# An inverse transform along W cut into four 64x64 products, with its sums and differences formed one stage earlier and its row sums on GpSimd

## The reference

```python
# x: (4, 128, 128, 768) f32; 8 channel blocks of 96; w1, w2: (2, 8, 96, 96); b1, b2: (2, 8, 96)
xf = jnp.fft.rfft2(x, axes=(1, 2), norm='ortho')            # 128 x 65 modes
o1r = relu(xr @ w1[0] - xi @ w1[1] + b1[0])                 # per mode and block
o1i = relu(xi @ w1[0] + xr @ w1[1] + b1[1])
o2r = softshrink(o1r @ w2[0] - o1i @ w2[1] + b2[0], 0.01)
o2i = softshrink(o1i @ w2[0] + o1r @ w2[1] + b2[1], 0.01)
out = jnp.fft.irfft2(o2r + 1j * o2i, s=(128, 128), axes=(1, 2), norm='ortho') + x
```

## Time and profile before

| | |
|---|---|
| runs of the kernel | 5120.54, 5124.18, 5125.72 us, median 5124.18 |
| profiled execution | span 5120.9 us (the profile gives no other time for it) |
| TensorE, its weight loads | busy 5023.2 us (98%), 4143.8 us (81%) |
| VectorE | 3992.9 us (78%) |
| ScalarE | 2512.6 us (49%) |
| GpSimd | 626.9 us (12%) |
| DMA | 421.11 MB, mean 82 GB/s |
| granted TensorE clock | 0.999 of full speed |

### The profile page before, as it was taken

The page is one execution under the profiler, slowest core; times in us unless marked ns, Lnnn a source line. Parts: engine busy times, 40 slices in busy tenths (PEclk is TensorE's granted clock), DMA queues, the critical chain, the costliest instruction groups (busy, mean ns, idle before and its releaser), DMA issues.

```text
span 5120.9 us, 112005 instructions
## 1 busy us (share of the span) xinstructions
PE 5023.2 (98%) x43200; PEld 4143.8 (81%) x43200; DVE 3992.9 (78%) x5987; ACT 2512.6 (49%) x3649; POOL 626.9 (12%) x420
## 2 busy tenths in 40 slices
PE   7999999999999999999999999999999999999999
PEld 6887878878788887888888888888878878888887
DVE  6778778787787877878777777777787777877877
ACT  4554545545455454554445544545545455454553
POOL 0111011110111101111011110011110111101111
PEclk9999999999999999999999999999999999999999
DMA  3331233312333123332133321333312333123311
GB/s 108 100 102 34 74 101 100 105 44 61 100 100 105 51 55 100 100 105 62 46 98 100 105 77 45 83 100 105 91 44 71 100 105 99 44 63 100 104 51 50
DMA packets 1067748, 421.11 MB, mean 82 GB/s; under 512 B 1064864, under 2 KB 1064992, under 8 KB 1067168
## 3 DMA queue, kind: packets, MB, share of 16 engines
q1 hardware_dynamic: 1062432, 411.63, 30.4%
q10 hardware_dynamic: 4736, 1.60, 0.1%
HBM read 210.26 MB, written 201.33 MB: 80 GB/s over the span
## 4 chain that ended last, share of the span: by engine, by line
issue 88%; POOL 12%; POOLq 0%; DVE 0%
POOL x L948 12%; POOLq L947 0%; POOLq L951 0%; DVE x L877 0%; POOLq L948 0%; POOLq L960 0%
## 5 line engine op out<-in xcount | busy, mean ns | idle before, releaser
L948 POOL TENSOR_TENSOR x<-shrink_or_v,x 128x480 f32<-128x480 f32 (+1 forms) x416 | 626.7, 1506 | 4485.8 <-DVE shrink_or_v L870 4445.1
L549 PE MATMUL ps<-wts,hbig 128*128 128x192 f32 x4160 | 732.1, 327 | 4.3
L842 DVE TENSOR_TENSOR shrink_or_v<-ps,wts 128x768 f32<-128x768 f32 (+1 forms) x544 | 501.1, 921 | 285.3 <-PE ps L558 258.6
L795 DVE COPY ydg<-ps 128x512 f32<-128x512 f32 (+5 forms) x768 | 504.7, 657 | 251.4 <-PE ps L453 151.7
L453 PE MATMUL ps<-tab,ring 128*128 128x128 f32 x6144 | 694.6, 276 | 4.2
L453 PEld LDWEIGHTS ps<-tab,ring 128*128 128x128 f32 x6144 | 688.5, 192 | 10.3 <-DVE ring L916 10.3
L549 PEld LDWEIGHTS ps<-wts,hbig 128*128 128x128 f32 x4160 | 673.2, 190 | 16.3 <-ACT hbig L710 13.7
L440 PE MATMUL ps<-tab,ring 128*64 128x128 f32 x6144 | 680.4, 273 | 3.3 <-ACT ring L650 3.3
L660 ACT COPY ydg<-ps 127x512 f32<-127x512 f32 (+5 forms) x896 | 503.0, 571 | 361.6 <-PE ps L453 185.3
L441 PE MATMUL ps<-tab,ring 128*63 128x128 f32 x6144 | 680.4, 273 | 0.0
L440 PEld LDWEIGHTS ps<-tab,ring 128*64 128x64 f32 x6144 | 671.3, 137 | 7.9 <-ACT ring L650 4.8
(11 more groups left out here) (79 smaller groups left out, 7581.0 us busy)
## 6 DMA issues: line engine op xcount, KB each, us to landing
out<-x SPq DMA_DIRECT2D x352, 480.0 KB, 4.6
x<-in_x SPq DMA_DIRECT2D x192, 768.0 KB, 7.6
x<-in_x SPq DMA_DIRECT2D x32, 816.0 KB, 7.8
x<-in_x SPq DMA_DIRECT2D x32, 720.0 KB, 6.4
out<-x SPq DMA_DIRECT2D x32, 432.0 KB, 4.2
wts<-in_mix SPq DMA_DIRECT2D x16, 513.0 KB, 3.6
out<-x SPq DMA_DIRECT2D x32, 240.0 KB, 4.4
out<-x SPq DMA_DIRECT2D x32, 192.0 KB, 4.3
```

Of the source, the lines that this page charges most:

```text
L549: mm = pe.matmul(o, hbig[:, k * H:(k + 1) * H], mix_part("w2_big"), start=first, stop=False, skip_group_check=True)
L795: dve.tensor_copy(*line_moves(stage, g)).then_inc(line_dve, 1)
L842: dve.tensor_tensor(parts(v), d, b2, ALU.add).then_inc(bias_done, 1)
L948: pool.tensor_tensor(xs[p][:, a:b, :], ucopy[g % 4][:, 0:b - a, :], mirror(xs[p], a, b), ALU.add).then_inc(plus_ready, 1)
```

## The change

The W transform of a real image has a symmetry between kw and 64-kw: for even w the cosines are equal and the sines opposite, for odd w the other way round. The change uses it in the inverse transform.

- `ydg` keeps kw 0 to 31 in its lower 64 slots and 32 and 64-kw in its upper 64; the groups of the mixing are now pairs (k, 64-k). The partitions of the image are reordered to even w, then odd w, so each load and each store is two transfers of 64 partitions (`load_x`, the stores).
- The ring slots of the inverse lines hold sums in one half and differences in the other. VectorE forms them with two operations a group (`mirror_sums`), ScalarE copies the four slots without a partner (`plain_slots`). For the first five slots `shrink` does it part by part during the mixing; L679 and L916 are gone.
- Each product of the rows stage becomes two of 64 input and 64 output partitions (`quarters`), four for a group.
- The difference to the mirror rows moves from VectorE to GpSimd, behind its own sum. `ucopy` has 13 buffers, which lie over those of the mixing, so the next unit's first copy of the mixing (`copy_big`) and its first shrink wait for GpSimd's last difference. Stores wait for GpSimd by batch.
- Packers and movers are shared out anew, and the folds are spread over rounds 1 to 6, two in round 1.

```diff
 def packer_a(g):
-    return "act" if g < RING + 2 or g % 3 == 2 else "dve"
-
-
-def packer_h(g):
-    return "act" if g < RING or g % 3 == 2 else "dve"
+    return "act" if g < RING + 2 or g % 3 != 1 else "dve"
...
 def mover(stage, g):
-    if stage == 0 and g < 4:
-        return "act"
-    return "dve" if g % 2 else "act"
+    if stage == 0:
+        return "act" if g < 4 or g % 4 == 2 else "dve"
+    return "dve" if g >= 21 and g % 2 else "act"
...
-GROUP_PAIRS = ([[(6, 7), (8, 9), (10, 11), (12, 13)], [(0, 64), (14, 15), (16, 17), (18, 19)]]
-               + [[(k + i, k + i + 1) for i in range(0, 8, 2)] for k in range(20, 60, 8)]
-               + [[(60, 61), (62, 63)], [(2, 3), (4, 5)], [(1, None)]])
+GROUP_PAIRS = [[(k, 64 - k) for k in ks] for ks in
+               [(1, 2, 3, 4), (0, 5, 6, 7)] + [range(k, k + 4) for k in range(8, 28, 4)] + [(28, 29), (30, 31)]]
+GROUP_PAIRS.append([(32, None)])
...
-FOLD_IN = {1: (0, 1, 2), 2: (3,), 3: (4,), 4: (5,), 5: (6,)}
...
+AREA = 60 * H + 28 * CB
...
+        ucopy = [over(f"ucopy{g}", [128, HG, CB], F32, area, AREA - (NF - g) * HG * CB) for g in range(NF)]
...
+        def batch_of(g):
+            return next(i for i, last in enumerate(STORE_AFTER) if g <= last)
+
+        def batch_part(g):
+
+            return 2 if g == NF - 1 else 1
+
+        def wait_batch(engine, q, g):
+            engine.wait_ge(batch_ready[batch_of(g)], 2 * q + 4)
 
         def line_moves(stage, g):
...
+        def mirror_sums(slots, to, a, b):
+
+            x, y = (ydg[:, o + 2 * a:o + 2 * b, slots].rearrange("p (k r) c -> p c k r", r=2) for o in (0, HALF))
+            to = to.rearrange("p c (t m) -> p c m t", t=2)
+            return (to[:, :, a:b, :], x, y), (to[:, :, 32 + a:32 + b, ::-1], x, y)
...
+        def plain_slots(slots, to):
+
+            return (to.rearrange("p c (t i m) -> p c i t m", t=2, i=2)[:, :, :, :, 0],
+                    ydg[:, :, slots].rearrange("p (i s) c -> p c i s", i=2)[:, :, :, 0:2])
+
+        def group_slots(g):
...
-            return ring[g % RING][:, 0:n, a:b], ydg[:, a:b, c:c + n].rearrange("p k c -> p c k")
+            return slice(c, c + n), ring[g % RING][:, 0:n, :]
...
                         for lo, hi in ((a, e + (e == HALF)), (H + 1 - e, H + 1 - max(a, 1))):
-                            sp.dma_start(xs[p][:, lo:hi, :], src[:, lo:hi, :]).then_inc(x_loaded[p][i], 16)
+                            for t in range(2):
+                                sp.dma_start(xs[p][t * HALF:(t + 1) * HALF, lo:hi, :],
+                                             src[t, :, lo:hi, :]).then_inc(x_loaded[p][i], 16)
...
-                            sp.wait_ge(y_ready, NF * q + NF + g + 1)
...
+                            for lo, hi in ((a, e), (H - min(e, H // 2) + 1, H - max(a, 1) + 1)):
+                                for i in range(2):
+                                    sp.dma_start(dst[i, :, lo:hi, :],
+                                                 xs[p][i * HALF:(i + 1) * HALF, lo:hi, :]).then_inc(stored[p], 16)
                             a = e
                         sp.wait_ge(stored[p], (t + 1) * 16 * STORES)
...
                             wait_moved(pe, q, 1, g - 8)
-                        who = packer_h(g)
-                        pe.wait_ge(pack_sems[who], PACKED_H[who] * q + upto(packer_h, g, who))
-                        if g < RING:
-                            pe.wait_ge(tail_packed, RING * q + g + 1)
+                        if g >= RING:
+                            pe.wait_ge(packed_dve, (NG - RING) * q + g - RING + 1)
+                            pe.wait_ge(packed_act, (NG - RING) * q + g - RING + 1)
+                        elif g == 0:
...
+                def quarters(g, cols):
+
+                    a, b = odd_rows(g)
+                    top, low = slice(0, HALF), slice(HALF, W)
+                    v, u = (ps[:, row_bank(g) + i, 0:n * CB].rearrange("p (h c) -> p h c", c=CB)[:, :, cols]
+                            for i, n in ((1, b - a), (0, HG)))
+                    yv, yu = ydg[:, HC + a - 1:HC + b - 1, cols], ydg[:, HG * g:HG * g + HG, cols]
+                    even, odd = mat("inv_w_even"), mat("inv_w_odd")
+                    pe.matmul(v[low], odd[top], yv[top], start=True, stop=True)
+                    mv = pe.matmul(v[top], odd[low], yv[low], start=True, stop=True)
+                    pe.matmul(u[top], even[top], yu[top], start=True, stop=True)
+                    mu = pe.matmul(u[low], even[low], yu[low], start=True, stop=True)
+                    return mv, mu
+
                 def rows(q, g):
-                    bank = row_bank(g)
                     if g >= 4:
...
-                    a, b = odd_rows(g)
...
-                              ydg[:, HC + a - 1:HC + b - 1, :].rearrange("p h c -> p (h c)"),
-                              start=True, stop=True).then_inc(v_done, 1)
-                    pe.matmul(ps[:, bank, 0:HG * CB], mat("inv_w_even"),
-                              ydg[:, HG * g:HG * g + HG, :].rearrange("p h c -> p (h c)"),
-                              start=True, stop=True).then_inc(u_done, 1)
+                        pe.sem_inc(row_banks_free, 1)
+                    mv, mu = quarters(g, slice(0, CB))
+                    mv.then_inc(v_done, 1)
...
 
                 def first_rows(q):
 
-                    a, b = odd_rows(0)
...
-                    v, u = (ps[:, row_bank(0) + i, 0:n * CB].rearrange("p (h c) -> p h c", c=CB)
-                            for i, n in ((1, b - a), (0, HG)))
-                    yv, yu = ydg[:, HC + a - 1:HC + b - 1, :], ydg[:, 0:HG, :]
                     lines_moved(q, 1, FIRST_LINES - 1)
-                    pe.matmul(v[:, :, 0:c], mat("inv_w_odd"), yv[:, :, 0:c], start=True, stop=True)
...
                 def pack(q, g):
                     act.wait_ge(line_done, lines_before(q, 1, g - RING) + 1)
-                    act.copy(*pack_moves(g)).then_inc(packed_act, 1)
+                    act.copy(*plain_slots(*group_slots(g))).then_inc(packed_act, 1)
...
+                    if u == 0 and h == 0:
+                        wait_batch(act, q - 1, NF - 1)
...
-                            if it == NU:
-                                early_pack(q, 0)
...
                         act.wait_ge(merge_done, q + 1)
+                        act.copy(rings[:].rearrange("p c (t m) -> p t c m", t=2)[:, :, 0:EARLY, 0],
+                                 ps[:, E_BANK, 0:2 * CB].rearrange("p (t c) -> p t c", t=2)[:, :, 0:EARLY]
+                                 ).then_inc(merged_packed, 1)
                         act.copy(ydg[:, 0:2, :].rearrange("p k c -> p (k c)"),
...
-                        for g in range(2, RING):
-                            early_pack(q, g)
...
                 def pack(q, g):
                     dve.wait_ge(line_done, lines_before(q, 1, g - RING) + 1)
-                    dve.tensor_copy(*pack_moves(g)).then_inc(packed_dve, 1)
+                    sums, differences = mirror_sums(*group_slots(g), 1, 32)
+                    dve.tensor_tensor(*sums, ALU.add)
+                    dve.tensor_tensor(*differences, ALU.subtract).then_inc(packed_dve, 1)
...
+                        e = parts(c)[:, :, 0, :]
+                        dve.tensor_tensor(e, parts(v)[:, :, 0, :], e, ALU.subtract).then_inc(edge_ready, 1)
+                        dve.wait_ge(edge_ready, q + 1)
+                        halves_of = edge[:].rearrange("p k (r c) -> p k r c", r=2)
+                        for r in range(2):
+                            pair = e[:, :, r * CB:(r + 1) * CB]
+                            dve.tensor_tensor(halves_of[:, r, r, :], pair[:, 0], pair[:, 1], ALU.add)
+                            dve.tensor_tensor(halves_of[:, 1 - r, r, :], pair[:, 0], pair[:, 1], ALU.subtract)
...
                     dve.tensor_tensor(dst, parts(v)[:, :, first:ne, :], parts(c)[:, :, first:ne, :],
                                       ALU.subtract).then_inc(shrunk, 1)
+                    dve.wait_ge(shrunk, NP * q + at)
+                    if at == 1:
+                        dve.wait_ge(line_done, lines_before(q, 1, 0))
+                    sums, differences = mirror_sums(slice(0, EARLY), rings[:], k, k + ne - first)
+                    dve.tensor_tensor(*sums, ALU.add)
+                    dve.tensor_tensor(*differences, ALU.subtract).then_inc(early_packed, 1)
...
-                    dve.scalar_tensor_tensor(ucopy[g % 4][:, 0:b - a, :], xs[p][:, a:b, :], 0.5, u[:, lo:lo + b - a, :],
+                    dve.scalar_tensor_tensor(ucopy[g][:, 0:b - a, :], xs[p][:, a:b, :], 0.5, u[:, lo:lo + b - a, :],
                                              ALU.mult, ALU.add).then_inc(uv_ready, 1)
-
-                def subtract(q, p, g):
-                    a, b = odd_rows(g)
-                    xm = mirror(xs[p], a, b)
-                    dve.wait_ge(plus_ready, NF * q + g + 1)
```

(63 more changed lines are left out.)

92 lines of the change are left out of this document (44 added, 48 removed).

## The result

The change made the kernel slower: 5307.98 us (median of 4 runs, 5302.66 to 5319.04) against 5123.49, a ratio of 1.036 (95% interval 1.035 to 1.038). The forecast was 4935, outside was also the range (up to 5200). The profiled execution has a span of 5305.3 us and a granted clock of 0.974, where it was 0.999.

What follows compares the result with a forecast made beforehand. TensorE's order of work was taken as the bound, VectorE close behind. Units of 95.65 + 56.9 = 152.55 us, 6.35 less, give -197 over 31 intervals; 5120.9 - 197 + 7 + 3.3 makes about 4935 us, range 4865 to 5200.

Steps and rivals of the forecast that it cites:

- Rival 1: Rows stage: the four products run only two abreast, 1.61 us a group; about 5123 us, no change; chance 0.12.
- rival 3: GpSimd's operations take 1.55 us instead of 1.22, so it ends at R + 42.6; about 5250 us; chance 0.05.
- I take the present rate, whose row is nearest: Loads and stores: transfers covering 64 partitions keep the present 0.28 MB/us, with the same packets and engines.
- 40.6 + 4.57/r: Time from R, a unit's start, to TensorE's group 3 through GpSimd, stores, loads and folds, at transfer rate r.
- Rival 2: Transfers of 64 partitions run below 0.221 MB/us; at 0.20 a unit takes 160.7 us, about 5200 us total; chance 0.23.
- The estimate of 5340 us: Total time if 64-partition transfers slow by the Trainium skill's ratio, 196 against 328 GB/s; set aside, as no row showed it.
- The 5800 us: Total time claimed if transfers ran at half the present rate, since even the stores would fall behind.
- Nothing, then: Inverse lines: the two-operation pack costs no time, some 0.7 us a group against TensorE's 0.9, cover 0.2 us.
- The price of 0.42 us: Inverse lines: each of VectorE's two pack operations of 248 elements, priced at 0.16 us + 1.04 ns an element.
- late folds alone: Every second unit, at VectorE's loop turn: folds started 4.60 us late, making the unit 160.1 us instead of 157.7.
- waits of under 3 us: TensorE's idle ahead of group 3, 2.2 us expected: a clock loss of 1.6 us counted only for waits over 3 us.
- 95.65: Microseconds from group 3 of the mixing to the next unit's start R: 95.4 - 0.6 + 0.85.

Runs made afterwards that it cites:

- Runs 1 to 3: In turn: changed kernel with 128-partition transfers (w in wrong order), 5090.9 us; kernel before with transfers cut by partitions, 5208.8 us; kernel before, cut by rows, 5116.6 us.
- run 12: Changed kernel with 128-partition transfers (w in wrong order) and all pack operations walked with the channel innermost: 4998.3 us, ratio 0.976.
- Run 9: Changed kernel without L829, the differences of the inverse lines' pack: 5259.2 us.
- run 10: Changed kernel with pack operations walked in another order, sums with the channel innermost, differences with the slot innermost: 5257.4 us.
- run 11: Changed kernel with early sums and differences on GpSimd and each fold a round later, pack of the inverse lines left on VectorE: 5026.2 us, ratio 0.982.

## Why the prediction was wrong

**What bounds the kernel, the rows stage, GpSimd: right.** Four quarters run abreast (0.81 us a group), VectorE paces at 1.13, L458 comes at R + 11.5 (forecast 11.6), GpSimd ends at R + 35.1 (34). Rival 1 fell with it: the Trainium skill's TensorEngine Tiling (Array Packing), "Gotcha 1: PSUM Pressure", has row tiles keep out of one PSUM bank at a time; here the two products of `v` share a bank on different partitions and start 0.04 us apart, so the trace decides against it for this form. GpSimd's operations beside VectorE's were 1.21 us (forecast 1.22), but 1.66 in several places once VectorE was in the forward lines; rival 3 took no hold.

**The step that failed first: "I take the present rate, whose row is nearest".** That row was near in packets, bytes and engines, and far in the one thing that the change altered. The rate of 64 partitions is 217 to 224 GB/s in the middle of a load, that of 128 is 323 at the same place and 281 in the earlier trace rows; over a whole load it is 0.20 and 0.28 MB/us. Runs 1 to 3 isolate it. The formula 40.6 + 4.57/r was right: at 0.20 it gives 63.5, and 64.1 was measured; at 0.28 it gives 56.9, and run 12 had 57.0. Rival 2 is what happened, with a price of 160.7 us a unit where 163.9 was measured. The Trainium skill's SBUF — State Buffer, "Door 1: The DMA port swizzle", gave 196 against 328 GB/s; the traces agree in kind, with 217 and 323. The estimate of 5340 us by that ratio stood nearer than the sum. The 5800 us that the prediction gives for half the rate has no working; its own formula gives about 5500.

**The second: "Nothing, then" for the pack.** The price of 0.42 us was read from operations whose operands lie in order, L852's in SBUF and one of L842's in PSUM. These read four channels at a stride of 384 bytes between slots, with the slot innermost, and held VectorE for 0.57 us each, 1.13 a group against TensorE's 0.9. The cover of 0.2 us a group was smaller than the error of the price. Run 9 shows the link, run 10 that the order of walking sets the price. With the channel innermost the forecast's 0.42 is nearly met (0.43 to 0.45), but not its 0.7 us a group: a pair takes 0.90, as much as TensorE's four channels, and the cover is nil.

**The sum.** Against the profiled execution the miss is 5305.3 - 4931 = 374 us. With both terms put back (run 12, span 4997.9) 307 of it are gone. Of the 67 left, 10 are my mean of the unit before: 31 intervals between the first R (173.5) and the last (5089.9) give 158.6 us, not 158.9. 44 are the 15 units behind the loop's turn, which I had taken as late folds alone (a row of the changed kernel):

```profile
1680.60 0.46 PE L458 MATMUL ps<-x,tab 128*128 128x96 f32 x2 [3.24 <-issue]
```

In them TensorE itself stands for 3.2 us ahead of L458, released by nothing that the profile shows, at the turn of its loop. Before, it was busy with the rows there until VectorE was done; with the products abreast it is not, and those units reach group 3 at R + 59.8 in run 12, with no wait there, instead of 57.0. What it waits for wasn't tested. The last 13 are the other units. Nine of them take 152.8 us; six take 154.7, as the granted clock is 0.84 over the 11 us behind their wait of 1.9 to 2.6 us at group 3. The forecast let waits of under 3 us pass without that cost.

In the changed kernel itself a unit is 11.3 us over the forecast: 6.9 up to group 3 (the rate) and 4.5 behind it.

**Rounds and the end of the mixing: right without the wait.** Forecast from group 3 to R 95.65, run 12 95.9 and 95.6 (medians). In the changed kernel it was 100.1. Of the 4.5 us more, 1.9 are the inverse lines and 1.8 the clock behind the wait at group 3, which rival 2 priced at 1.6. 0.5 are the end of the mixing, 1.4 us longer than before where 0.85 was forecast, and 0.3 are R, which came 0.3 us sooner and not 0.6. The 1.8 are not the folds: two units of the trace with the same folds kept the full clock, and took 73.7 us from group 3 to the first L489, as the last unit did (73.6), which has neither wait nor folds. All others took 75.0 to 76.6. Windows of 11 us from group 3 on, the first behind a wait of 9.25 us, the second, in one of the two, behind 1.94:

```profile
3867.05:3878.05 11.00, 10.99 (x61) 9.42 (x61) 9.24 (x13) 2.64 (x4) 0.00 (x0) 0.73 0.92 156
4031.25:4042.25 11.00, 11.00 (x85) 9.20 (x86) 10.54 (x15) 3.99 (x6) 0.00 (x0) 1.00 0.92 163
```

With the clock at 0.73 the same 11 us hold 61 of TensorE's passes instead of 85.

## What to carry to other kernels

Look at what an edit changes that no row of the trace has, and take as neighbour the row that shares that, or none: here the partitions of a transfer (load 31.3 us instead of 22.5) and the order in which a two-operand operation walks strided elements (0.57 us instead of 0.45). A wait on a load belongs late in an in-order engine's program, behind what others wait for: folds a round later and the early operations on GpSimd gave 282 us (run 11) with the slow loads left in, more than the fast loads alone (217). Before an operation is put on an engine as "hidden", compare its cover (0.2 us a group) with the uncertainty of its price.

## What was not expected of the hardware

- A transfer issued from ScalarE's queue held ScalarE: 21.4 us for seven transfers of some 384 KB while SyncE's queue was loading too.
- GpSimd took 1.51 us for a strided operation of 248 elements with two operands in SBUF and 1.21 us for 480 in order beside VectorE's row additions; VectorE's operation beside the first grew from 0.62 to 1.10 us. The Trainium skill's SBUF — State Buffer, "Who interferes with whom", has the two engines share one pair of ports that one of them holds at a time; VectorE's two durations agree with that.
- Mean durations of overlapping operations mislead: 0.67 us of duration, 0.57 from start to start. For a pace, read the starts.
